# A fused attention and feed-forward block: x on another queue, its second load in one transfer a half, columns and G in another order

## The reference

```python
x = L0_attn_x                                            # (4, 4096, 512)
xn = _layernorm(x, axis=-1)
x = x + _L0_attn_ref(xn, ...) + _L0_ffn_ref(xn, ...)

# feed-forward branch: 64 features of 16 inner units each
s = einsum('btd,dm->btm', xn, Win) + bin_
h = relu(s[..., None] * W1 + b1)                         # (b, t, 64, 16)
g = einsum('btmh,mh->btm', h, W2) + b2
out = einsum('btm,md->btd', g, Wout) + bout
```

## Time and profile before

| | |
|---|---|
| median of 3 runs | 387.22 us (387.07 to 390.45) |
| the profiled execution | 386.97 us, its span 385.2 us |
| TensorE busy | 318.6 us (83%) |
| VectorE busy | 273.1 us (71%) |
| ScalarE busy | 224.0 us (58%) |
| GpSimd busy | 235.8 us (61%) |
| mean granted TensorE clock | 0.932 of 2.4 GHz |
| moved by DMA | 87.80 MB, 228 GB/s |

### The profile page before, as it was taken

One profiled execution on the slowest core, in us unless ns is written; L12 is line 12 of the kernel. 1 busy time (PEld: TensorE's weight loads), 2 busy tenths in 40 slices (PEclk: granted clock), 3 DMA queues, 4 the chain that ended last, 5 costly groups with the idle time before them and its releaser, 6 DMA issues.

```text
span 385.2 us, 5266 instructions
## 1 busy us (share of the span) xinstructions
PE 318.6 (83%) x1804; PEld 150.0 (39%) x1804; DVE 273.1 (71%) x422; ACT 224.0 (58%) x278; POOL 235.8 (61%) x209
## 2 busy tenths in 40 slices
PE   4775999788799999997998795949869594899784
PEld 3452554544246344533343242413324241343322
DVE  2779766788898999699983856737395672886534
ACT  1464756437477657575677473735746374578750
POOL 9535938429629693966757390936629093487950
PEclk9998799899699999999999698987969899799999
DMA  8993977644384946557495665848556494462468
GB/s 238 323 406 97 268 238 279 239 172 175 117 287 175 344 172 223 229 208 284 175 322 192 182 244 196 319 173 285 212 186 261 172 339 172 173 260 114 186 154 327
DMA packets 49834, 87.80 MB, mean 228 GB/s; under 512 B 5625, under 2 KB 34449, under 8 KB 45713
## 3 DMA queue, kind: packets, MB, share of 16 engines
q1 hardware_dynamic: 48384, 86.93, 63.1%
q0 software_dynamic: 640, 0.16, 0.7%
q10 hardware_dynamic: 784, 0.39, 0.5%
HBM read 53.77 MB, written 33.69 MB: 227 GB/s over the span
## 4 chain that ended last, share of the span: by engine, by line
SPq 50%; PE 24%; DVE 13%; DMA 5%; issue 5%; ACT 2%; DVEq 0%; ACTq 0%
SPq L245 43%; PE op L537 7%; PE s L478 5%; PE g L515 4%; SPq L237 4%; DVE x L912 3%; DMA x<-in_L_attn_x_dram 3%; SPq L254 3%; DMA xq<-in_L_attn_x_dram 2%; PE T L457 2%; DVE stats L939 2%; DVE w2s L785 2%; PE rep L499 1%; ACT H L667 1%; PE op L340 1%
## 5 line engine op out<-in xcount | busy, mean ns | idle before, releaser
L667 ACT ACTIVATE H<-rep,b1c,w1c 128x1024 f32<-128x1024 f32 x128 | 146.5, 1212 | 53.0 <-PE rep L499 45.5
L1046 POOL TENSOR_TENSOR x<-x,bias_row 128x512 f32<-128x512 f32 x128 | 161.6, 1302 | 5.1 <-DVE bias_row L776 5.1
L912 DVE TENSOR_TENSOR x<-x,op 128x1024 f32<-128x1024 f32 x62 | 75.1, 1212 | 32.9 <-PE op L537 32.9
L1030 POOL TENSOR_TENSOR rstd<-veps,nhalf 128x8 f32<-128x8 f32 x16 | 26.4, 1649 | 104.0 <-DVE veps L949 104.0
L939 DVE BATCH_NORM_STATS2 stats<-x 128x6 f32<-128x512 f32 x128 | 80.7, 679 | 7.8 <-DMA x<-in_L_attn_x_dram 7.6
L537 PE MATMUL op<-wout,G 64*128 64x512 f32 x248 | 81.5, 736 | 5.3 <-DVE x L912 5.3
L922 DVE STREAM_TRANSPOSE xqT<-xq 128x1024 f32<-128x1024 f32 x28 | 34.8, 1241 | 54.7 <-DMA xq<-in_L_attn_x_dram 38.8
L642 ACT ACTIVATE xT<-T 128x512 f32<-128x512 f32 x60 | 36.0, 601 | 50.8 <-PE T L457 50.7
L478 PE MATMUL s<-xT,win 128*64 128x512 f32 x128 | 63.4, 641 | 0.8 <-ACT xqT L642 0.8
L515 PE MATMUL g<-H,w2s 128*32 128x512 f32 x512 | 63.7, 607 | 0.4 <-ACT H L667 0.4
L478 PE MATMUL s<-xqT,winq 128*64 128x512 f32 x112 | 56.2, 648 | 0.0
(11 more groups left out here) (170 smaller groups left out, 301.7 us busy)
## 6 DMA issues: line engine op xcount, KB each, us to landing
x<-in_L_attn_x_dram SPq DMA_DIRECT2D x32, 1024.0 KB, 9.9
out_dram<-x SPq DMA_DIRECT2D x30, 1024.0 KB, 6.2
xq<-in_L_attn_x_dram SPq DMA_DIRECT2D x224, 64.0 KB
out_dram<-x SPq DMA_DIRECT2D x4, 512.0 KB, 3.2
x<-in_L_attn_Wq_dram SPq DMA_DIRECT2D x1, 1024.0 KB, 17.5
x<-in_L_attn_Wk_dram SPq DMA_DIRECT2D x1, 1024.0 KB, 19.6
x<-in_L_attn_Wv_dram SPq DMA_DIRECT2D x1, 1024.0 KB, 7.6
x<-in_L_attn_Wo_dram SPq DMA_DIRECT2D x1, 1024.0 KB, 10.2
```

The source lines that it names most:

```text
L667: act.activation(Hr[half][k % len(Hr[half])][:, :], rep_ps[:, :], ACT.Relu, bias=b1c[:, half, k:k + 1], scale=w1c[:, half, k:k + 1]).then_ ...
L912: dve.tensor_tensor(both, both, sum_banks(n, j)[:, :].rearrange("p (h d) -> p h d", h=2), ALU.add).then_inc(add_done, 1)
L1046: pool.tensor_tensor(x_sb[m][:, c], x_sb[m][:, c], bias_row[:, :], ALU.add).then_inc(xc_done, 1)
```

## The change

- `load_quads` issues one transfer of 512 KB instead of eight of 64 KB. The view of x is taken apart differently: column block i, then 256 tokens in order. A partition now holds 8 tokens that follow each other, where it held tokens 32 apart.
- The columns of block 1 therefore come to `s_product` in another order, and its output is written through a rearranged view of `s_ps` (step 8), so that it stands in token order again.
- Pairs 6 to 15 are loaded by `load_pair` on ScalarE's queue, in body n between `s_high(n-1)` and `evacuate(n, 2)`, in one transfer of 2 MB; ScalarE waits there for the two stores of pair n-4. Pairs 0 to 5 stay on SyncE's.
- Wv and Wo go ahead of quads 0 and 1 on SyncE's queue.
- Two entries of `AT_DVE`, the copies of turned weight parts 4 and 6, move from body 2 to the end of body 1.
- `evacuate_g` writes G in tile order and reads `g_ps` at a step of 4; `project` takes 128 columns that follow each other.

```diff
-    xq_v = x.rearrange("b (n h t a) (i d) -> (b n) h i a t d", h=2, t=BLK // QD, a=QD, d=P)
+    xq_v = x.rearrange("b (n u k) (i d) -> (b n) u i k d", u=4, k=QD * QH, d=P)
...
+        ldp = [sem(f"ldp{r}") for r in range(RING)]
...
         AT_DVE = iter((
-            -32, -32, -32, 34, 34, 36, 39, 39, 39, 39, 41, 48, 66, 66, 69, 69, 71, 74, 74, 74, 79, 80, 96, 98, 99,
+            -32, -32, -32, 34, 34, 36, 39, 39, 39, 39, 41, 48, 48, 48, 69, 69, 71, 74, 74, 74, 79, 80, 96, 98, 99,
...
-            elif n >= RING and h == 0:
-                for i in range(2):
-                    queue.wait_ge(st[m][i], 16 * (n // RING))
-            queue.dma_start(x_sb[m][:, h * HALF:(h + 1) * HALF], x_v[n, h, :, :]).then_inc(ld[m][h], 16)
+            sp.dma_start(x_sb[m][:, h * HALF:(h + 1) * HALF], x_v[n, h, :, :]).then_inc(ld[m][h], 16)
+
+        def load_pair(n):
 
             m = n % RING
+            for i in range(2):
+                act.wait_ge(st[m][i], 16 * (n // RING))
+            act.dma_start(x_sb[m][:, :].rearrange("p (h d) -> p h d", h=2), x_v[n, :, :, :].rearrange("h p d -> p h d")).then_inc(ldp[m], 16)
+
+        def landed(n, h):
+
+            return (ld[n][h], 16) if n < RING else (ldp[n % RING], 16 * (n // RING))
 
         def load_quads(k):
...
-            for t in range(QH):
-                sp.dma_start(xq[r][:, t * P:(t + 1) * P], xq_v[n, 1, :, :, h * QH + t, :]).then_inc(ldq[r], 16)
+            sp.dma_start(xq[r][:, :], xq_v[n, 2 + h, :, :, :]).then_inc(ldq[r], 16)
...
+            load_weight(2, Wv)
+            load_weight(3, Wo)
             load_quads(0)
             load_quads(1)
-            load_weight(2, Wv)
-            load_weight(3, Wo)
...
-                if n + AHEAD >= RING and has(n + AHEAD):
-                    for h in range(2):
-                        load(sp, n + AHEAD, h)
                 if has(n + 1):
                     load_quads(2 * (n + 1 - BY_PE) + 1)
...
-                    pe.wait_ge(ld[m][b], 16 * (n // RING + 1))
+                    pe.wait_ge(*landed(n, b))
...
-                    mm = pe.matmul(s_ps[b * M:(b + 1) * M, :], w[:, c, :], turned_x, start=(c == 0), stop=(c == DC - 1))
+                    own = s_ps[b * M:(b + 1) * M, :]
+                    if b == 1 and n >= BY_PE:
+                        own = own.rearrange("m (h a t) -> m h t a", h=2, t=QH)
+                    mm = pe.matmul(own, w[:, c, :], turned_x, start=(c == 0), stop=(c == DC - 1))
...
-                mm = pe.matmul(sum_banks(n, j)[:, b * D:(b + 1) * D], G[n % 2][own, j::TILES], wout[own, :],
+                mm = pe.matmul(sum_banks(n, j)[:, b * D:(b + 1) * D], G[n % 2][own, j * P:(j + 1) * P], wout[own, :],
...
-            act.activation(G[n % 2][:, :], g_ps[:, :], ACT.Identity, bias=b2c[:, 0:1]).then_inc(g_made, 1)
+            act.activation(G[n % 2][:, :].rearrange("m (j p) -> m j p", j=TILES), g_ps[:, :].rearrange("m (p j) -> m j p", j=TILES), ACT.Identity, bias=b2c[:, 0:1]).then_inc(g_made, 1)
...
                 if has(n - 1):
                     s_high(n - 1)
+                if n + AHEAD >= RING and has(n + AHEAD):
+                    load_pair(n + AHEAD)
                 reach(side, n, 7)
                 if has(n):
                     evacuate(n, 2)
```

More of the change, by code:

```diff
@@ L29, in residual_block @@
     BLK = TPP // 2 * P
+    QH = BLK // QD // 2
     PAIR = 2 * BLK
@@ L44, in residual_block @@
     NV = 5
-    QH = BLK // QD // 2
     x_v = x.rearrange("b (n h p j) d -> (b n) h p (j d)", h=2, p=P, j=TPP // 2)
     out_v = out.rearrange("b (n h p j) d -> (b n) p h (j d)", h=2, p=P, j=TPP // 2)
-    xq_v = x.rearrange("b (n h t a) (i d) -> (b n) h i a t d", h=2, t=BLK // QD, a=QD, d=P)
+    xq_v = x.rearrange("b (n u k) (i d) -> (b n) u i k d", u=4, k=QD * QH, d=P)
     pe, act, dve, pool, sp = nc.tensor, nc.scalar, nc.vector, nc.gpsimd, nc.sync
@@ L222, in residual_block, with load @@
         HALF = TPP // 2 * D
-        def load(queue, n, h):
-            m = n % RING
[L228 to L233, removed]
-            elif n >= RING and h == 0:
-                for i in range(2):
-                    queue.wait_ge(st[m][i], 16 * (n // RING))
-            queue.dma_start(x_sb[m][:, h * HALF:(h + 1) * HALF], x_v[n, h, :, :]).then_inc(ld[m][h], 16)
+        def load(n, h):
+            m = n
+            if n == 3 and h == 0:
+                sp.wait_ge(turned, 2 * DC)
+            elif n == 4 and h == 0:
+                sp.wait_ge(qk_ps, 1)
+            elif n == 5 and h == 0:
+                sp.wait_ge(turned, 4 * DC)
+            sp.dma_start(x_sb[m][:, h * HALF:(h + 1) * HALF], x_v[n, h, :, :]).then_inc(ld[m][h], 16)
+        def load_pair(n):
+            m = n % RING
+            for i in range(2):
[3 more added lines that the diff above has]
+            return (ld[n][h], 16) if n < RING else (ldp[n % RING], 16 * (n // RING))
         def load_quads(k):
@@ L261, in sp_program @@
             sp.dma_start(win[:, :, :], Win.rearrange("(c p) m -> p c m", p=P)).then_inc(in_win, 16)
[L262 to L265, removed]
+            load(0, 0)
+            load(0, 1)
+            load(1, 0)
+            load(1, 1)
             sp.dma_start(bias_row[:, :], bout.partition_broadcast(P)).then_inc(in_rows, 16)
@@ L269, in sp_program @@
             load_weight(1, Wk)
-            load(sp, 2, 0)
-            load(sp, 2, 1)
+            load(2, 0)
+            load(2, 1)
+            load_weight(2, Wv)
+            load_weight(3, Wo)
             load_quads(0)
             load_quads(1)
-            load_weight(2, Wv)
-            load_weight(3, Wo)
             sp.dma_start(wout[0:M, :], Wout).then_inc(in_wo2, 16)
@@ L285, in sp_program @@
                 sp.dma_start(scal[:, i:i + 1], v.partition_broadcast(P)).then_inc(in_scal, 16)
-            load(sp, 3, 0)
-            load(sp, 3, 1)
+            load(3, 0)
+            load(3, 1)
             load_quads(2)
[L289 to L292, removed]
+            load(4, 0)
+            load(4, 1)
+            load(5, 0)
+            load(5, 1)
             for n in range(2, BODIES):
@@ L918, in turn_quads @@
             k = 2 * (n - BY_PE) + h
-            dve.wait_ge(ldq[k % 3], 16 * QH * (k // 3 + 1))
+            dve.wait_ge(ldq[k % 3], 16 * (k // 3 + 1))
             if h == 0:
@@ L937, in statistics @@
             if j % 4 == 0:
-                dve.wait_ge(ld[m][j // 4], 16 * (n // RING + 1))
+                dve.wait_ge(*landed(n, j // 4))
             dve.bn_stats(stats[:, j, :], x_sb[m][:, j * D:(j + 1) * D]).then_inc(bn_done, 1)
```

## The result

The changed kernel takes **421.06 us** (median of 5 runs, 420.10 to 425.87) against 387.22 before: a ratio of **1.088, interval 1.080 to 1.096**. It is slower by 34 us, far outside the predicted range. Its profiled execution, the slowest of the five, took 425.87 us (span 424.0).

The account below looks back on a forecast made before the run. Four of 16 DMA engines, full with quads, were taken as the bound from 149 to 321 us. Terms -1, +0.5, +2.5 and -2.5 sum to -0.5 us: forecast 387 us, no change, range 379 to 396.

Parts of the forecast that it names:

- the bound: From 149 to 321 us, four of 16 DMA engines carry all quads and are full; period 22.84 us.
- Rival A: Line 245: the new quad transfer spreads over all 16 engines and compute becomes the bound, 338 us; chance 0.09.
- the same bytes in the same 512 B runs … 23.0 ns for one: Line 245, quads in one transfer a half: only completion packets go, 0 to -2.3 us, taken as -1.
- The bytes go over the same 16 engines, so the four full ones gain nothing: Loads of x on ScalarE's queue: only ten issues there count, +0.5 us, bounds 0 and 8.5.
- rival B: ScalarE's issue of x is held behind SyncE's transfers and it goes on late: 403 to 426 us; chance 0.09.
- the stall: ScalarE waits about 6 us for the stores of pair n-4, hidden by VectorE's wait for quads, cost 0.
- the start: Wv and Wo ahead of quads on SyncE: load of pair 3 at 53.5 at most, +2.5 us, bounds 0 and +5.
- G: Tile order: packed loads 147 ns instead of 316 in projects where compute paces, 0 to -6.8 us, taken as -2.5.

Follow-up runs that it names:

- tile_writes: The changed kernel with a half of quads again in eight transfers, each into one block of 128 columns, rows of x placed as changed: 395.71 us, 1.020.

## Why the prediction was wrong, step by step

- **Right: the bound.** Four engines full of quads were the limit, and stayed it: share 0.30 with quads alone, and 0.87 of the time once they spread. Rival A had the right size (338 us against 336.85) for a change that the diff did not make. Beside it I quoted the advice to coalesce; its words are on transfers under 64 KB, and those of before are 64 KB each. Followed here, it cost 3.9%.
- **Wrong, the step that failed: "the same bytes in the same 512 B runs … 23.0 ns for one".** I carried the price of a run over from eight transfers to one, and looked only at the source. The destination's order changed: before, an engine wrote once into a partition and went on; now it writes eight times there. The term was -1; alone it measured +15 us (3.9%, 3.0 to 4.8), at 71 GB/s instead of 86. With the old order of writes put back (tile_writes), 25 us of the 34 were gone. That it is engines 32 partitions apart, in step, that collide is argued. The bounds of 0 to -2.3 came from completions only. The page of before could not show the new price, and I should have said so and bounded it.
- **Wrong: "The bytes go over the same 16 engines, so the four full ones gain nothing", +0.5.** It counted bytes and not what runs at once. On one queue, loads of x and quads are taken in order; on two they overlap. With the old form this cost 2.3 us, inside the bounds of 0 to 8.5. With the new form it cost 17. Two edits, each costed by itself, had a price together.
- **Right in mechanism, rival B wrong: the stall.** ScalarE's issue was never held, and its wait for the stores is hidden:

```profile
240.35 0.37 ACTq L242 DMA_DIRECT2D x<-in_L_attn_x_dram  x1
240.82 0.60 ACT L650 ACTIVATE xT<-T 128x512 f32<-128x512 f32 x1 [4.19 <-DMA out_dram<-x]
```

  The issue takes 0.37 us (at most 0.39 in all ten), the idle time before it is 4.19 where I had about 6, and VectorE still waits for quads after it (7.41 at 254.07). B's 403 to 426 us held the result by luck: its mechanism did not happen.
- **Size off: the start.** SyncE's order in the changed kernel:

```profile
20.77 18.58 SPq L253 DMA_DIRECT2D xq<-in_L_attn_x_dram  x2
39.40 6.40 SPq L284 DMA_DIRECT2D wout<-in_L_ffn_Wout_dram  x1
...
52.91 0.90 SPq L235 DMA_DIRECT2D x<-in_L_attn_x_dram  x2
```

  The load of pair 3 moved to 52.91 (at most 53.5 predicted). The term of +2.5 with its bound of +5 measured +5.2 (2.6 to 7.7): so about the whole bound arrived.
- **Size off: G.** The load of G fell by 100 to 114 ns and not by 169, and of the -2.5 us came -0.6 (-1.9 to +0.6). I had counted projects in the stretches that compute paces; there too the gain did not show in the time.
- **The sum.** -1, +0.5, +2.5 and -2.5 should have read +15, +17 (beside the new form; +2 by itself), +5 and -1: 36, where 34 were measured. Nothing in my range had a price for an altered order of writes: every case but B held the four engines' time for a byte fixed.

## What to carry to other kernels

Before two transfers are called the same bytes, compare both orders, at the source and at the destination: which partition each engine writes next, for how many writes it stays, and (the likely reason here) which other engine writes 32 partitions from it at that time. When engines are full, look at GB/s beside the share of busy time: 0.65 for 203 where it was 0.64 for 231 says that the price of a byte rose, which no count of bytes shows. And where four engines of 16 carry the load, change the outermost dimension first; issuing less (+3.9%) or on another queue (+0.6%) gained nothing here, and spreading alone was worth 11%, with the rest of the change 13%.

## What the chip showed that I had not expected

- Four engines that write rows into 64 or 128 partitions can slow down with no other transfer in flight: 64 and 69 GB/s against 87 for the same bytes into 32 partitions. It need not happen: the 128-partition form had 87 in another run. Beside a load of x it is 65 ns against 27 for a 512-byte packet, and the load's own 8 KB packets take 570 ns against 324.
- Who starts first decides. A load of x that starts ahead of quads costs them only its own time (35.5 to 36.5 us for three halves beside three pairs, in all forms on four engines); with one that meets quads under way the forms differ, 24.5 against 19.7.
- Copies from device memory to device memory did not disturb either form beyond their own time (20.3 and 20.9 us).
- Open: why the load of x itself slows to 527 ns on engines that carry no quads. The copy from tile to tile slows the same way, so it lies on the side of the writes; which engine blocks which was not tried. Open too: why eight writes in a row with engines 4 partitions apart took 22.2 us, and whether it is the distance or the number of partitions that spares the 32-partition form. A form for this kernel with a half's quads on four engines 8 partitions apart was not tried either: the turn on VectorE wants each block of columns on its own 32 partitions.
